# Softmax sums over the keys by VectorE's block transposition in the first 56 quarters, not by TensorE's products with ones; their output projections five double steps later

## The reference

```python
q = jnp.einsum('bsd,dhk->bshk', x, Wq) + bq        # x: the normalised input
k = jnp.einsum('bsd,dhk->bshk', x, Wk) + bk
v = jnp.einsum('bsd,dhk->bshk', x, Wv) + bv
q = q / jnp.sqrt(jnp.asarray(depth, q.dtype))
attn = jnp.einsum('bqhd,bkhd->bhqk', q, k)
attn = jax.nn.softmax(attn, axis=-1)
out = jnp.einsum('bhqk,bkhd->bqhd', attn, v)
return jnp.einsum('bqhd,hdm->bqm', out, Wo) + bo
...
x = x + _layernorm(attention(_layernorm(x)))
x = x + _layernorm(ffn(_layernorm(x)))
```

## Time and profile before

| | before |
|---|---|
| median of 3 runs | 2379.71 us (2378.05 to 2379.79) |
| the profiled execution | 2382.51 us |
| its span | 2380.7 us |
| TensorE busy | 2341.8 us, 98% |
| VectorE busy | 2066.7 us, 87% |
| ScalarE busy | 1380.4 us, 58% |
| GpSimd busy | 2112.9 us, 89% |
| share of the chain that ended last | TensorE 95%, VectorE 2% |
| granted TensorE clock, mean | 0.991 |

### The profile page before, as it was taken

The page is one execution under the profiler, slowest core; times in us unless marked ns, Lnnn a source line. Parts: engine busy times, 40 slices in busy tenths (PEclk is TensorE's granted clock), DMA queues, the critical chain, the costliest instruction groups (busy, mean ns, idle before and its releaser), DMA issues.

```text
span 2380.7 us, 43479 instructions
## 1 busy us (share of the span) xinstructions
PE 2341.8 (98%) x15632; PEld 1181.5 (50%) x15632; DVE 2066.7 (87%) x3166; ACT 1380.4 (58%) x1672; POOL 2112.9 (89%) x1210
## 2 busy tenths in 40 slices
PE   6999999999999999999999999999999999999998
PEld 3445455545555455454554545554554545544454
DVE  7888888888888888888888888888888888889977
ACT  6655556565555655555555655656556565655545
POOL 6888989989889988989989898988989898899986
PEclk8999999999999999999999999999999999999999
DMA  2000001000000000100000000100000000110101
GB/s 59 28 14 28 28 15 32 28 15 28 28 19 28 28 16 26 33 22 20 28 22 25 28 28 15 32 28 15 28 28 19 28 28 15 35 32 19 37 28 36
DMA packets 63895, 62.54 MB, mean 26 GB/s; under 512 B 29796, under 2 KB 47588, under 8 KB 63684
## 3 DMA queue, kind: packets, MB, share of 16 engines
q1 hardware_dynamic: 62820, 59.51, 8.5%
q10 hardware_dynamic: 864, 0.26, 0.0%
HBM read 56.88 MB, written 2.61 MB: 25 GB/s over the span
## 4 chain that ended last, share of the span: by engine, by line
PE 95%; DVE 2%; POOL 1%; issue 1%; ACT 0%; DMA 0%; POOLq 0%; DVEq 0%; ACTq 0%
PE o_ps L455 38%; PE spare_ps L410 14%; PE score_ps L434 10%; PE score_ps L440 10%; PE score_ps L437 10%; PE spare_ps L396 3%; PE spare_ps L500 3%; PE spare_ps L387 3%; PE spare_ps L378 3%; PE spare_ps L467 1%; DVE max_part L895 1%; POOL total L1177 1%; DVE ln_stats L867 0%; PE spare_ps L480 0%; PE score_ps L548 0%
## 5 line engine op out<-in xcount | busy, mean ns | idle before, releaser
L1177 POOL TENSOR_TENSOR total<-total,probs 128x832 f32<-128x832 f32 (+1 forms) x896 | 1761.5, 1966 | 225.1 <-ACT probs L722 151.9
L895 DVE TENSOR_REDUCE max_part<-spare_ps 128x1 f32<-128x512 f32 x2027 | 1303.3, 685 | 266.0 <-PE spare_ps L410 251.8
L722 ACT ACTIVATE probs<-score_ps 128x1024 f32<-128x1024 f32 x1024 | 993.0, 1022 | 815.0 <-PE score_ps L440 814.9
L455 PE MATMUL o_ps<-probs,v_sb 128*64 128x512 f32 x4096 | 980.8, 599 | 0.0
L455 PEld LDWEIGHTS o_ps<-probs,v_sb 128*64 128x64 f32 x4096 | 266.4, 136 | 451.4 <-issue 280.6
L410 PE MATMUL spare_ps<-k_hi,q_hi 64*128 64x512 f32 x2027 | 462.6, 450 | 8.9 <-DVE max_part L895 4.4
L410 PEld LDWEIGHTS spare_ps<-k_hi,q_hi 64*128 64x128 f32 x2027 | 194.0, 184 | 429.6 <-issue 228.6
L434 PE MATMUL score_ps<-q_hi,kd_hi 64*128 64x512 f32 x2048 | 407.1, 393 | 0.0
L440 PE MATMUL score_ps<-q_hi,kd_lo 64*128 64x512 f32 x2048 | 405.1, 391 | 0.0
L437 PE MATMUL score_ps<-q_lo,kd_hi 64*128 64x512 f32 x2048 | 404.4, 390 | 0.0
L938 DVE TENSOR_REDUCE part_sum<-probs 128x192 f32<-128x768 f32 (+1 forms) x255 | 392.7, 1540 | 0.7 <-ACT probs L722 0.7
(11 more groups left out here) (142 smaller groups left out, 1167.1 us busy)
## 6 DMA issues: line engine op xcount, KB each, us to landing
m_all<-m_scratch SPq DMA_DIRECT2D x64, 512.0 KB, 4.4
denom<-denom_scratch SPq DMA_DIRECT2D x122, 128.0 KB, 2.9
m_scratch<-neg_rows SPq DMA_DIRECT2D x256, 1.0 KB
y_acc<-in_L_attn_x SPq DMA_DIRECT2D x8, 256.0 KB, 6.1
key_f<-in_L_attn_x SPq DMA_DIRECT2D x8, 256.0 KB, 2.8
...
denom_col<-denom SPq DMA_DIRECT2D x61, 4.0 KB
denom_scratch<-denom_col SPq DMA_DIRECT2D x61, 4.0 KB, 1.4
```

The lines of the kernel that those rows point to most:

```text
L455: last = nc.tensor.matmul(o_ps[half(h), :], v_sb[:, b, kt, half(h)], probs[:, st % RING, h, :], start=(kt == 0), stop=(kt == T - 1))
L722: nc.scalar.activation(probs[:, st % RING], score_ps[st % 2][:], ACT.Exp, scale=SCALE).then_inc(s["exp_done"], 1)
L895: nc.vector.reduce_max(max_part[:, G % 2, h, qt, kc:kc + 1], bank[max_bank(n, h)], AX.X).then_inc(s["max_done"], 1)
L1177: nc.gpsimd.tensor_tensor(others(total[:, G % 2], G), so_far, others(probs[:, st % RING], G), ALU.add).then_inc(s["sum_done"], 1)
```

## The change

For the first 56 quarters (`TURNED`) the sum over the partitions is taken without TensorE. VectorE transposes `total` in blocks of 32 by 32 (`dve_turn`, in d = 4 of the next quarter), so that 32 keys of a block come to lie along a row; it sums each row's 32 neighbours, which leaves 128 partitions by 32 numbers, and transposes these (`dve_row_sums`, d = 0 of the quarter after that). Each block of 32 partitions then holds a quarter of every query's sum. Four transfers of 4 KB (`sp_quarters`, d = 1) lay the four parts side by side in `denom_quarters`; VectorE adds them and takes the reciprocal (`dve_quarters`, d = 2), and from there the way is the old one: to the scratch and back (`sp_denom_back`, now d = 2 in place of 5), GpSimd's `norm` (d = 5 of the second quarter after, in place of d = 7 of the next), and the output projection with VectorE's addition (d = 6 in place of 1 of the second quarter after). ScalarE's copy and one bank of the ring for each quarter go. The quarters from 56 on are as before.

```diff
+TURNED = CHUNKS - 2 * NC
+TURN_AT, ROW_SUM_AT, QUARTERS_OUT_AT, QUARTERS_AT, TURNED_NORM_AT, TURNED_WO_AT = 4, 0, 1, 2, 5, 6
...
-    if d == WO_AT and 2 <= G < CHUNKS + 2 - COLUMN_CHUNKS:
+    if d == (TURNED_WO_AT if G - 2 < TURNED else WO_AT) and G - 2 < CHUNKS - COLUMN_CHUNKS:
...
-        if d == L_AT and 0 < G <= CHUNKS - COLUMN_CHUNKS:
+        if d == L_AT and by_products(G - 1):
             use("L", G - 1)
...
+        def dve_turn(dve, G):
+            dve.wait_ge(s["sum_done"], (G + 1) * ADDS)
+            dve.wait_ge(s["merge_done"], G + 1)
...
+            nc.vector.transpose(q_parts[:].rearrange("p c n -> p (c n)"),
+                                total[:, G % 2].rearrange("p h n -> p (h n)")).then_inc(s["sums_turned"], 1)
+
+        def dve_row_sums(dve, G):
+            dve.wait_ge(s["sums_turned"], G + 1)
...
+            nc.vector.tensor_reduce(row_sum[:], q_parts[:].rearrange("p c (b i) -> p (c b) i", i=32), AX.X, ALU.add).then_inc(s["rows_summed"], 1)
+            dve.wait_ge(s["rows_summed"], G + 1)
...
+            nc.vector.transpose(row_turned[:], row_sum[:]).then_inc(s["rows_turned"], 1)
+
+        def dve_quarters(dve, G):
+            dve.wait_ge(s["quarters_in"], 64 * (G + 1))
...
+            nc.vector.tensor_reduce(denom_col[:], denom_quarters[:].rearrange("p a k -> p k a"), AX.X, ALU.add).then_inc(s["quarters_added"], 1)
+            dve.wait_ge(s["quarters_added"], G + 1)
+            nc.vector.reciprocal(denom_col[:], denom_col[:]).then_inc(s["recip_done"], 1)
...
+                if d == QUARTERS_AT and by_blocks(G - 2):
+                    dve_quarters(dve, G - 2)
+                if d == RECIP_AT and by_products(G - 1):
                     dve_recip(dve, G - 1)
...
+                if d == TURN_AT and by_blocks(G - 1):
+                    dve_turn(dve, G - 1)
+                if d == ROW_SUM_AT and by_blocks(G - 2):
+                    dve_row_sums(dve, G - 2)
...
+                if d == TURNED_NORM_AT and by_blocks(G - 2):
+                    norm(pool, G - 2)
...
+        def sp_quarters(sp, G):
+            sp.wait_ge(s["rows_turned"], G + 1)
...
+            for a in range(P // 32):
+                sp.dma_start(denom_quarters[:, a, :], row_turned[a * 32:(a + 1) * 32, :]).then_inc(s["quarters_in"], 16)
```

More of the change, by code:

```diff
@@ L107, in projected_at, with by_products, by_blocks @@
 def projected_at(G, d):
-    if d == WO_AT and 2 <= G < CHUNKS + 2 - COLUMN_CHUNKS:
+    if G < 2:
+        return None
+    if d == (TURNED_WO_AT if G - 2 < TURNED else WO_AT) and G - 2 < CHUNKS - COLUMN_CHUNKS:
         return G - 2
     return None
+def by_products(G):
+    return TURNED <= G < CHUNKS - COLUMN_CHUNKS
+def by_blocks(G):
+    return 0 <= G < TURNED
 def ffn_at(n, stage):
@@ L206, in build @@
         denom_4 = sb("denom_4", [P, CH // 2])
+        row_sum = sb("row_sum", [P, 32])
+        row_turned = sb("row_turned", [P, 32])
+        denom_quarters = sb("denom_quarters", [P, P // 32, 2 * TC])
         denom_col = sb("denom_col", [P, CH // HD])
@@ L348, in take @@
                 elif was == "L":
-                    pe.wait_ge(s["denom_copied"], k + 1)
+                    pe.wait_ge(s["denom_copied"], k + 1 - TURNED)
                 elif was == "Wo":
@@ L730, in act_denom @@
         def act_denom(act, G):
-            act.wait_ge(s["denom_ps_ready"], G + 1)
-            if G:
-                act.wait_ge(s["col_dma"], 16 * G)
+            act.wait_ge(s["denom_ps_ready"], G + 1 - TURNED)
+            if G > TURNED:
+                act.wait_ge(s["col_dma"], 16 * (G - TURNED))
             nc.scalar.activation(denom_4[:], bank[SPARE["L", G]][:, 0:CH // 2], ACT.Copy).then_inc(s["denom_copied"], 1)
@@ L940, in dve_part, with total_taken @@
                                     AX.X, ALU.add).then_inc(s["part_done"], 1)
+        def total_taken(eng, G):
+            if by_blocks(G):
+                eng.wait_ge(s["sums_turned"], G + 1)
+            else:
+                eng.wait_ge(s["denom_ps_ready"], G + 1 - TURNED)
+        def dve_turn(dve, G):
+            dve.wait_ge(s["sum_done"], (G + 1) * ADDS)
+            dve.wait_ge(s["merge_done"], G + 1)
+            if G:
+                dve.wait_ge(s["rows_summed"], G)
+            else:
+                dve.wait_ge(s["first_split"], 2)
+            nc.vector.transpose(q_parts[:].rearrange("p c n -> p (c n)"),
+                                total[:, G % 2].rearrange("p h n -> p (h n)")).then_inc(s["sums_turned"], 1)
+        def dve_row_sums(dve, G):
+            dve.wait_ge(s["sums_turned"], G + 1)
+            if G:
+                dve.wait_ge(s["rows_turned"], G)
+            nc.vector.tensor_reduce(row_sum[:], q_parts[:].rearrange("p c (b i) -> p (c b) i", i=32), AX.X, ALU.add).then_inc(s["rows_summed"], 1)
+            dve.wait_ge(s["rows_summed"], G + 1)
+            if G:
+                dve.wait_ge(s["quarters_in"], 64 * G)
+            nc.vector.transpose(row_turned[:], row_sum[:]).then_inc(s["rows_turned"], 1)
+        def dve_quarters(dve, G):
+            dve.wait_ge(s["quarters_in"], 64 * (G + 1))
+            if G:
+                dve.wait_ge(s["scratch_dma"], 16 * G)
+            nc.vector.tensor_reduce(denom_col[:], denom_quarters[:].rearrange("p a k -> p k a"), AX.X, ALU.add).then_inc(s["quarters_added"], 1)
+            dve.wait_ge(s["quarters_added"], G + 1)
+            nc.vector.reciprocal(denom_col[:], denom_col[:]).then_inc(s["recip_done"], 1)
         def dve_merge(dve, G):
@@ L1100, in dve_program @@
                     dve_centre(dve)
-                if d == RECIP_AT and 0 < G <= CHUNKS - COLUMN_CHUNKS:
+                if d == QUARTERS_AT and by_blocks(G - 2):
+                    dve_quarters(dve, G - 2)
+                if d == RECIP_AT and by_products(G - 1):
                     dve_recip(dve, G - 1)
@@ L1171, in pool_add @@
                 if G >= 2:
-                    pool.wait_ge(s["denom_ps_ready"], G - 1)
+                    total_taken(pool, G - 2)
                 so_far = others(probs[:, (st - 1) % RING], G)
@@ L1291, in pool_program @@
                 G, u, c, d = n // PER_CHUNK, n // (PER_CHUNK * NC), n // PER_CHUNK % NC, n % PER_CHUNK
-                if d == NORM_AT and 0 < G <= CHUNKS - COLUMN_CHUNKS:
+                if d == TURNED_NORM_AT and by_blocks(G - 2):
+                    norm(pool, G - 2)
+                if d == NORM_AT and by_products(G - 1):
                     norm(pool, G - 1)
@@ L1407, in sp_program @@
                     sp_ffn_weights(sp)
-                if d == DENOM_OUT_AT and 0 < G <= CHUNKS - COLUMN_CHUNKS:
+                if d == QUARTERS_OUT_AT and by_blocks(G - 2):
+                    sp_quarters(sp, G - 2)
+                if d == QUARTERS_AT and by_blocks(G - 2):
+                    sp_denom_back(sp, G - 2)
+                if d == DENOM_OUT_AT and by_products(G - 1):
                     sp_denom_out(sp, G - 1)
```

16 lines of the change are left out of this document (10 added, 6 removed).

## The result

| | before | after |
|---|---|---|
| median | 2379.75 us (6 runs, 2378.05 to 2380.49) | 2389.43 us (6 runs, 2387.05 to 2392.64) |
| ratio after to before | | 1.004, 95% interval 1.003 to 1.005 |
| the profiled execution, its span | 2382.51, 2380.7 us | 2389.42, 2387.3 us |

What follows compares the result with a forecast made beforehand. TensorE, busy 98% and waiting for VectorE's row maxima, was taken as the bound. Four kinds of quarter averaged +0.165 us, times 56 = +9.2 us, giving 2389 us for the median; 8-in-10 range 2362 to 2437 us.

Steps and rivals of the forecast that it cites:

- a: Offset from TensorE's first product of a double to VectorE's first maximum; double grows by a - 0.78 (0.73 with projection).
- What leaves TensorE: Four products with ones leave double 3, 0.58 us; double 7 loses its 0.13 us and takes 3.91.
- The partial sum in a bare double: VectorE's 1.46 us partial sum with four maxima overfills a double without projection; doubles 2 and 4 grow to 4.97 and 4.01.
- The transposition: VectorE's 1024-column block transposition in double 4 takes 1.25 us; a = 1.14 in double 5, which takes 5.19.
- The row sum: VectorE's sum of 1024 to 32 in double 0 takes 1.22 us; behind keys a = 1.26 in double 1.
- Double 0: Double 0 stays at 3.91 us; its new VectorE work gives a = 0.89 in double 1, which grows to 4.00.
- Transfers: Four small transfers issued in double 1 land within 2.9 us, before VectorE's small sum in double 2; wait priced at nothing.
- VectorE's idle: VectorE's idle time before the row maxima falls by about 150 us.
- the slow rate: Rival: transposition or sum runs at the strided 2 ns an element, +47 us each, 2436 or 2483 us; chance 0.13.
- Short passes: Rival: both large VectorE passes take near 1.0 us, about -0.28 us a quarter, -16 us, 2364 us; chance 0.15.
- The clean gain: Rival: VectorE's idle 4.2 us a quarter takes the 2.9 new ones, TensorE never waits; -40 us, 2340 us; chance 0.08.
- Late transfers: Rival: four small transfers land 0.5 us after VectorE asks, delaying second pairs of maxima; +28 us, 2417 us; chance 0.12.

## Why the prediction was right

The forecast was +9.2 us; the distances between the doubles give +8.3 and the medians +9.7. The mechanism is shown: the slack is in the wrong place, and each double whose maxima begin late grows, with a slope near 1 from a = 0.89 to 2.19. That the total came so close is luck in part. The four kinds of quarter (without keys; with keys in double 4; with keys in 0 and 4; with keys in 4 again) were forecast at +0.10, +0.11, +0.44 and +0.01 and came to +0.01, +0.15, +0.47 and -0.04: errors of up to 0.09 that nearly cancel. The +0.44 doesn't follow from its own terms, which add up to about +0.51 (the +0.11 of the second kind, 0.38 more in double 1, 0.02 more in double 5).

- **What leaves TensorE.** 0.58 in double 3 and 0.13 in double 7: 3.91 both. The sum had double 3 at 3.95, for an a of 0.84; it was 0.72.
- **The partial sum in a bare double.** Doubles 2 and 4 were forecast at 4.97 and 4.01 and took 4.95 and 4.02. The move alone (+8.5) and the products away (10 us short of 32.5, 9.0 of them in double 4) show this term without any of the new passes.
- **The transposition.** 1231 ns for a forecast 1.25. Double 5 was forecast at 5.19 and took 5.11: the passes between the maxima of double 4 and of double 5 follow each other closer than I had added up (1.06 in place of 1.14). That is 0.08 too large in the 14 quarters without keys, 1.1 us; with keys a was 1.05, 1.07 and 0.95 for a forecast 1.04, 1.06 and 1.0. The small transposition in its place shows its price, 16.7 us.
- **The row sum.** 1208 ns for 1.22. Behind keys a was 1.17 and double 1 took 4.27, for a forecast 1.26 and 4.39, worked out from the earlier trace rows; there too the passes follow each other closer: from the end of the key difference to the first maximum 1.29 us passed, for 1.39.
- **Double 0: the step that failed.** The prediction let double 7 give back its 0.13 and double 0 stay at 3.91 ("Double 0: 3.36 + 1.22 + 0.22 = 4.80, less 3.91, a = 0.89 in double 1, which grows by 0.1 to 4.00"). Double 0 took 4.01, for ScalarE's seed, and double 1, whose maxima were therefore at 0.82 rather than 0.89, took 3.92. The sum of the two, 7.93, is the 7.91 forecast: two errors that cancel by luck, so the time could not tell; the halved seed (-7.0 us with double 0 at 3.91 to 3.92) and the small row sum (double 0 still 4.01) did. In quarters with keys in double 0 both losses stand: 4.86 and 4.27.
- **Transfers.** Landed 1.8 us after issue (median), against the 2.9 taken as the bound. That nothing had to be paid was right.
- **GpSimd.** Double 6 took 4.80 and 4.77 to 4.79 in the other kinds, so its projection does not wait for the normalisation; no wait of the projection for GpSimd stands in the trace.
- **VectorE's idle** before the maxima fell by 126 us, for 150 forecast.

Of the rivals, the slow rate fell with the two durations. "Vector Engine (DVE) Microarchitecture Reference", section 3.8, of the Trainium skill, one element per cycle and lane for a transposition, is borne out at this size in that 1231 ns for 1024 columns is the pace of a plain contiguous pass (1217 for the seeding), where 2 ns a column would have been 2.1 us. By "SBUF — State Buffer", section "Door 1: The DMA port swizzle", of the same skill the contiguous sum should run at full rate, and it does: 1208 ns for 1024 against 1538 for the strided 768. Short passes fell too, 1.21 and 1.23 against the 1.0 they needed. The clean gain was wrong by 49 us, though VectorE still idles 140 us ahead of its maxima: idle time ahead of second pairs can't be spent ahead of first ones. Late transfers fell with the 1.1 us.

What the parts come to: the move costs 8.5 us. To exchange the products for VectorE's passes on top of it costs 1.4 more (2389.43 - 2387.99): 32.5 us saved, 16.7 given back for the transposition, 7.4 for the row sum. The 9.8 left over lie in double 4, behind a double 3 that is now bare: with keys it takes 4.95 to 4.96 in the kernel after and 4.76 to 4.77 with the move alone, without keys 4.02 for about 3.91; (3 x 0.18 + 0.11)/4 x 56 = 9.1 us. The kernel without the products lost the same there. Each of these prices is a difference of two medians whose ratios are known to about 0.1%, so it may be off by 2 to 3 us; the row sum's 7.4 is 4.9 by the doubles.

Open: what lies between the totals. The medians differ by 9.7 us, the two profiled executions by 6.9 and their spans by 6.6: +8.1 in the 52 quarters, -1.5 in all the rest. The profiled execution of the kernel before was 2.8 us above its median, at a granted clock of 0.991; that of the kernel after was at its median, at 0.993. Whether the clock explains all of it isn't shown.
